# Flamingo block with a routed FFN: scaling behind the next tile's copies, order flags per distance, two buffers for the shared activations

## The reference, cut to what matters

```python
# x: 16 x 128 tokens of 256 features, ctx: 16 x 128 x 256
x = x + tanh(g_xattn) * xattn(layernorm(x), ctx)      # 16 heads of 64, one shared K/V head
                                                      # + a parallel silu(gate) * h feed-forward of 1024
x = x + tanh(g_ffn) * ffn(layernorm(x))

def ffn(x):
    shared = silu(x @ sh_up_w + sh_up_b) @ sh_down_w + sh_down_b
    scores = softmax(x @ gate_w.T)                    # 8 experts
    topk_w, topk_i = top_k(scores, 2)                 # weights normalised over the two
    for each token, each chosen expert e:
        y += w_e * (silu(x @ up_w[e] + up_b[e]) @ down_w[e] + down_b[e])     # 256 -> 256 -> 256
    return y + shared
```

## Time and profile before

| | |
|---|---|
| median of the runs | 539.51 us |
| profiled execution | 539.47 us |
| its span in the trace | 537.8 us |
| PE busy | 503.8 us (94%) |
| DVE / ACT / POOL busy | 409.4 / 327.1 / 288.5 us |
| from 446 to 524 us (78 us): PE / DVE / ACT / POOL busy | 74.25 / 57.16 / 49.04 / 55.95 us |
| granted TensorE clock in that stretch | 1.00 |
| share of the DMA engines in that stretch | 0.73 |

### The profile page before, as it was taken

How to read it: one execution, slowest core, us unless ns; L and a number is a source line. 1 busy time by engine, 2 the same in 40 slices (tenths; PEclk the granted TensorE clock), 3 DMA queues, 4 the chain that set the end, 5 groups by cost and what they waited for, 6 DMA issues and landing times.

```text
span 537.8 us, 13926 instructions
## 1 busy us (share of the span) xinstructions
PE 503.8 (94%) x4026; PEld 485.3 (90%) x4026; DVE 409.4 (76%) x1254; ACT 327.1 (61%) x1092; POOL 288.5 (54%) x330
## 2 busy tenths in 40 slices
PE   8789999999999999999999999999998889999980
PEld 7779999999999999999999999999997779889870
DVE  7687878688787878878887878787778887777760
ACT  3576656766675666566567565756665636666650
POOL 3487626454552655264355536444676315488763
PEclk9889999999999999999999999999999999999995
DMA  5551300021003000300301030023598965688853
GB/s 176 189 188 50 99 2 32 31 78 52 31 20 117 31 30 14 114 32 20 117 22 33 7 122 26 10 79 100 198 320 331 380 229 107 112 128 137 134 69 39
DMA packets 40212, 53.85 MB, mean 100 GB/s; under 512 B 4597, under 2 KB 34218, under 8 KB 39146
## 3 DMA queue, kind: packets, MB, share of 16 engines
q1 hardware_dynamic: 31856, 41.48, 23.2%
q0 software_dynamic: 8000, 11.86, 11.9%
q10 hardware_dynamic: 314, 0.01, 0.0%
HBM read 28.15 MB, written 25.21 MB: 99 GB/s over the span
## 4 chain that ended last, share of the span: by engine, by line
PE 66%; DVE 15%; issue 6%; ACT 5%; POOL 3%; DMA 2%; DVEq 1%; SPq 0%; POOLq 0%; ACTq 0%
PE bank L1523 14%; PE bank L1525 12%; PE bank L1524 12%; PE bank L1604 5%; PE bank L1709 4%; PE bank L1616 4%; PE bank L1699 4%; PE bank L1620 3%; PE bank L1607 2%; PE bank L1714 2%; PE bank L1538 2%; DVE norm_probs L988 2%; ACT norm_probs L803 1%; DMA spare<-in_L_xattn_Wq 1%; POOL weights L587 1%
## 5 line engine op out<-in xcount | busy, mean ns | idle before, releaser
L616 POOL TENSOR_TENSOR norm_probs<-norm_probs,rden 128x512 f32<-128x512 f32 x64 | 66.5, 1040 | 100.0 <-DVE rden L1168 99.2
L1523 PE MATMUL bank<-acts,weights 128*128 128x256 f32 x384 | 110.1, 287 | 3.4 <-POOL weights L587 3.4
L1524 PE MATMUL bank<-acts,weights 128*128 128x256 f32 x384 | 108.7, 283 | 0.0
L1525 PE MATMUL bank<-acts,weights 128*128 128x256 f32 x384 | 108.4, 282 | 0.0
L803 ACT ACTIVATE norm_probs<-bank,nmax 128x128 f32<-128x128 f32 x256 | 90.4, 367 | 23.4 <-DVE nmax L1124 23.4
L621 POOL TENSOR_TENSOR acts<-uf,acts 128x256 fp32r<-128x256 f32 x64 | 47.5, 741 | 68.7 <-ACT acts L791 68.7
L1523 PEld LDWEIGHTS bank<-acts,weights 128*128 128x128 f32 x384 | 73.3, 191 | 4.1 <-issue 3.0
L727 POOL DMA_INDIRECT out_x<-norm_probs,th x39 | 60.8, 1558 | 29.3 <-ACT norm_probs L916 16.7
L1525 PEld LDWEIGHTS bank<-acts,weights 128*128 128x128 f32 x384 | 73.2, 191 | 0.0
L1524 PEld LDWEIGHTS bank<-acts,weights 128*128 128x128 f32 x384 | 73.1, 190 | 0.0
L791 ACT ACTIVATE acts<-uf 128x256 fp32r<-128x256 f32 x64 | 26.8, 418 | 61.8 <-DVE uf L1193 61.7
(11 more groups left out here) (250 smaller groups left out, 1567.1 us busy)
## 6 DMA issues: line engine op xcount, KB each, us to landing
parked<-stage SPq DMA_DIRECT2D x12, 512.0 KB, 3.5
weights<-parked SPq DMA_DIRECT2D x6, 1024.0 KB
slot_rows<-tf SPq DMA_DIRECT2D x8, 680.0 KB, 6.5
spare<-slot_rows SPq DMA_DIRECT2D x39, 136.0 KB
ct<-in_ctx SPq DMA_DIRECT2D x8, 256.0 KB, 2.7
xs<-in_x SPq DMA_DIRECT2D x8, 256.0 KB, 4.5
stage<-in_L_ffn_up_w SPq DMA_DIRECT2D x8, 256.0 KB, 2.8
stage<-in_L_ffn_down_w SPq DMA_DIRECT2D x8, 256.0 KB, 3.1
```

The source lines that it names most:

```text
L616: pool.tensor_tensor(pr[:, s % 2], pr[:, s % 2], rden[:, s % 2, :].unsqueeze(2).broadcast_to((P, 4, P)), ALU.mult).then_inc(probs_ready, 1)
L1523: pe.matmul(ps, wts[1], mov[0], start=first, stop=False, skip_group_check=True)
L1524: pe.matmul(ps, wts[0], mov[0], start=False, stop=False, skip_group_check=True)
L1525: return pe.matmul(ps, wts[0], mov[1], start=False, stop=last, skip_group_check=True)
```

## The change

Line numbers in the diff are those of the files; behind the last attention group and in the tile loop nearly every engine's order moves.

- ScalarE's tile step scales last but one: rows t+2, hidden t-1, then `ys` of t-3, then Silu.
- Waits that other waits imply are left out (`tile_down_filled`, `hT_filled` on ScalarE; `tile_silu_done`, most of `y_copied` on VectorE; `tile_biased`, `down_biased`, `xg_ready` from tile 3 on TensorE).
- One flag becomes two, per distance: `turns[0]` for the tile just before, `turns[1]` for the one before that, packed into a code per expert and unpacked by shifts. GpSimd loads both per tile, and waits for `y_copied` last. With the given inputs `turns[0]` is 0 everywhere, and `turns[1]` is 16 at tiles 6 and 8 (by the kernel's formula).
- `hf` has two buffers. The low part of the last shared step moves to GpSimd, behind the row sends. `expert_lo(0)` and `(1)` move one slot forward, to slots 4 and 5.
- VectorE behind attention: `hidden_lo(1)` before the logits' copy, `add_shared(0)` before the tables. The first part of the flag table, the first register load and the first two `meta` come before the first tile's bias.

```diff
-        hf = xn.rearrange("p a n -> p (a n)").rearrange("p (m n) -> p m n", m=KT)
+        hf = norm_probs.rearrange("p s (m n) -> p s m n", m=KT)
...
@@ gpsimd
-                    if s in (5, 6) and last:
-                        expert_lo(s - 5)
+                    if s in (4, 5) and last:
+                        expert_lo(s - 4)
...
+            for m in range(KT):
+                step = TPS - 1
+                pool.wait_ge(hh_done, step * KT + m + 1)
+                pool.tensor_tensor(hh[:, step % 2, 1, m, :], hf[:, step % 2, m, :], hh[:, step % 2, 0, m, :].bitcast(F32),
+                                   ALU.subtract).then_inc(last_h_ready, 1)
...
             for t in range(TILES):
-                pool.wait_ge(y_copied, t + 1)
                 if t == 1:
                     pool.wait_ge(turns_done, 1)
                 if t >= 1:
-                    due = pool.value_load(turn[0:1, t:t + 1], min_val=0, max_val=16)
+                    due_1, due_2 = [pool.value_load(turns[i][0:1, t:t + 1], min_val=0, max_val=16) for i in range(2)]
                 if t >= 3:
                     pool.wait_ge(y_added[(t - 3) % 4], 16 * ((t - 3) // 4) + 32)
                 if t >= 2:
-                    pool.wait_ge(y_added[(t - 2) % 4], due + (16 * ((t - 2) // 4) + 16))
+                    pool.wait_ge(y_added[(t - 2) % 4], due_2 + (16 * ((t - 2) // 4) + 16))
                 if t >= 1:
-                    pool.wait_ge(y_added[(t - 1) % 4], due + (16 * ((t - 1) // 4) + 16))
+                    pool.wait_ge(y_added[(t - 1) % 4], due_1 + (16 * ((t - 1) // 4) + 16))
...
+                pool.wait_ge(y_copied, t + 1)
...
@@ scalar, hidden_hi
-                    if step > 0:
-                        act.wait_ge(h_ready, step * KT + m - KT + 1)
+                    if step >= 2:
+                        act.wait_ge(h_ready, (step - 2) * KT + m + 1)
...
@@ vector, behind attention
             x1_lo(g, dn_ps[USE_X1T % 4]).then_inc(dn_freed, 1)
+            hidden_lo(1)
...
-            hidden_lo(1)
+            add_shared(0)
+            hidden_lo(2)
...
             tables()
-            hidden_lo(2)
-            add_shared(0)
-            hidden_lo(3)
             add_shared(1)
...
@@ vector, tile_step
+                if t == -1:
+                    turn_table(0)
+                    dve.wait_ge(tables_done, 2)
+                    experts_of = dve.value_load(window[0:1, 0:1])
+                    for n in range(2):
+                        pick_meta(n, n)
+                if t in (0, 1):
+                    turn_table(t + 1)
...
@@ tensor, tile_step
-                    if t >= 2:
-                        pe.wait_ge(tile_biased, t - 1)
-                    pe.wait_ge(xg_ready, t + 1)
+                    if t < 3:
+                        pe.wait_ge(xg_ready, t + 1)
...
-                    if t >= 4:
-                        pe.wait_ge(down_biased, t - 3)
```

More of the change, by code:

```diff
@@ L205, in program @@
         weight = route(4).rearrange("p (t c) -> p t c", t=2)
-        hist = [route(NE), route(NE)]
+        hist_t = route(2 * NE).rearrange("p (k e) -> p k e", k=2)
+        hist = [hist_t[:, k, :] for k in range(2)]
         weight8 = routing[:, 0:4 * NE].rearrange("p (t c e) -> p t c e", t=2, c=2)
@@ L240, in program @@
         shares = consts[0:1, 486:486 + WIN_TILES]
-        late, early = consts[0:1, 494:494 + NE], consts[0:1, 502:502 + NE]
+        late_early = consts[0:1, 494:494 + 2 * NE].rearrange("p (k e) -> p k e", k=2)
+        late, early = [late_early[:, k, :] for k in range(2)]
         meta = th[:, 0:2 * TILES].rearrange("p (t n) -> p t n", n=2)
@@ L251, in program @@
         by_expert = slow_stage[0:1, 0:NTAB * (NE - 1)].rearrange("p (t e) -> p t e", e=NE - 1)
-        turn_f, floor_0, floor_1, shared_turn = [slow_stage[0:1, 320 + 48 * i:320 + 48 * i + (NE if i else NTAB)]
-                                                 for i in range(4)]
+        turn_f = slow_stage[0:1, 320:320 + NTAB]
+        turn_code = consts[0:1, 326:326 + NTAB].bitcast(I32)
+        floor, near = [slow_stage[0:1, 368 + 16 * i:368 + 16 * (i + 1)].rearrange("p (k e) -> p k e", k=2) for i in range(2)]
+        far, code = [slow_stage[0:1, 400 + 8 * i:408 + 8 * i] for i in range(2)]
+        turns = [slow_stage[0:1, 416 + 48 * i:416 + 48 * i + NTAB].bitcast(I32) for i in range(2)]
         count_i, count_t = slots8[0:1, 0, 0, :], slots8[0:1, 0, 1, :]
@@ L370, in program @@
         h_ready = sem("h_ready")
+        last_h_ready = sem("last_h_ready")
         dn_filled = sem("dn_filled")
@@ L1503, in tile_step @@
                                       hsT[0][(c + 1) % 2][:, :, :].bitcast(F32), ALU.subtract).then_inc(hT_ready, 1)
-                if runs(t + 2):
-                    e = dve.snap((experts_of >> (SHIFT * (k + 4))) & (NE - 1))
-                    dve.tensor_copy(meta[:, t + 2, :], rows_g[:, (c + 2) % 4, bass.ds(e * 2 + D, 2)]
-                                    ).then_inc(meta_ready, 1)
+                if t < 0:
+                    add_shared(3, (t + 2,))
+                if t == -1:
[6 more added lines that the diff above has]
+                    turn_table(t + 1)
+                if t >= 0 and runs(t + 2):
+                    pick_meta(t + 2, k + 4)
                 if runs(t - 2):
```

80 lines of the change are left out of this document (41 added, 39 removed).

## The result

The changed kernel took 543.17 us (median of 20 runs, 541.27 to 546.09); the kernel before took 539.95 beside it (20 runs). The ratio is 1.0059, 95% interval 1.0046 to 1.0073: slower by 0.6%. The forecast was 533.1, its range 531.0 to 537.3. The profiled execution took 542.22 with a span of 540.0.

What follows compares the result with a forecast made beforehand. Bound: the tile loop's ScalarE-VectorE ring, 2.05 us a step, GpSimd's scatters second. Tile 5 at 448.2, plus 33 x 1.95, 8.7 tail and 0.5: last scatter 521.8, 6.4 earlier; 539.5 - 6.4 = 533.1 us, range 531.0 to 537.3.

Steps and rivals of the forecast that it cites:

- Part 1, the pace: Tile loop: scaling behind both copies brings 2.15 us per tile to 1.95, 6.7 us less over 33 tiles.
- Part 2: Waits left out because other waits imply them: costed at nothing, at most 0.1 us in all.
- Part 3, the flags: GpSimd's scatters: distance-1 waits at tiles 5 and 8 go, 6.2 us; new waits at tiles 6 and 8 cost 2.8.
- Part 3, the second load: GpSimd's second register load per tile: taken to hide in the 1.55 us of the scatter before, cost 0.
- My other bound: GpSimd's second load: path of 1.8 us against 1.55 to hide in, so 0.15 to 0.25 per scatter.
- the equal gaps of 0.30: GpSimd: back-to-back scatters with a load lie as far apart as row sends without one, so loads hide.
- The rival with it, at 537.0: Second load on GpSimd shows in part: 0.15 per scatter, period 2.01, 537.0 us; chance 0.16.
- Part 4, the slots: Last attention group: moving GpSimd's subtractions one slot forward ends a TensorE stall, net 0.7 us less; bounds +0.3 and -1.0.
- Part 5: Behind attention: TensorE's 1.72 us stall goes but gives nothing; 0.2 later, stores may slow first row loads by up to 0.8.
- Part 6, the entrance: Front of tile loop: VectorE's flag work, load and copies delay the first bias; 0.8 us later at tile 5, bounds 0 and 1.8.
- first bias later than 441.5: Sign in the changed profile that would count against the forecast; VectorE's first bias was expected near 440.2.
- Two chains of equal length: Last scatter at 521.3 by TensorE's chain, 521.2 by GpSimd's; 0.5 us added for the tie.

Runs made afterwards that it cites:

- one_load: Changed kernel with one register load per tile on GpSimd instead of two, the distance-1 flag being a constant 0; 537.44 us (ratio 0.9968).
- old_flags: Changed kernel without register loads in the scatter loop, constant flags making tiles 5 and 8 wait for both t-1 and t-2, as before; 542.31 us (1.0047).
- slots_alone: shared_back with GpSimd's weight subtractions of the last attention group at slots 4 and 5 instead of 5 and 6; 535.22 us (0.9907).
- slots_back: packed_back with GpSimd's weight subtractions of the last attention group back at slots 5 and 6; 537.91 us (0.9965).
- shared_back: packed_back with the whole order of the shared experts' part as before, slots 5 and 6 included; 535.25 us (0.9911).
- meta_back: Changed kernel with the tile loop's entrance order as before: VectorE's load, first copies and flag table, and TensorE's load; 540.78 us (1.0012).
- packed_back: Changed kernel with both flags in one word, so one GpSimd load per tile, and meta_back's entrance order; 536.19 us (0.9924).
- loop_only: Kernel before with only ScalarE's new tile-loop order and the left-out waits of the change; 539.02 us (0.9987).

## Why the prediction was wrong

The dates of the sum against those of the changed kernel: tile 4's scatter 455.2, measured 459.95 (+4.75); from tile 4 to tile 8 10.2, measured 10.64 (+0.44); 30 scatters 55.8, measured 59.91 (+4.1); less the 0.6 by which the forecast's last scatter lay above GpSimd's own 521.2. That is the 8.7 by which the last scatter missed its date (521.8, measured 530.50). The tail was 9.5 for the 9.64 taken. The rest to 10.1 is the span's surroundings (2.2 for 1.67) and the profiled execution lying 0.95 below its median. Of the 4.75, 3.9 are TensorE's entrance (tile 5's up-projection at 452.06, forecast 448.2), and the remaining 0.9 is the second load again, by the 8.53 against one_load's 7.59.

- **Part 1, the pace: right.** 1.95 expected, 1.90 measured. The sum gained nothing by it, as GpSimd bound the end.
- **Part 2: nothing speaks against it.** No row shows a wait in place of what was left out; it was not tried by itself.
- **Part 3, the flags: right.** Waits of 5.84 and 4.80 between starts for 5.11 each; the sum had 6.2 - 2.8 = 3.4 us for them, old_flags gives 4.8, uncertain by 1.3.
- **Part 3, the second load: the step that failed.** It was taken at 0 and cost 0.14 a tile, 4.1 us behind tile 8 by the profile and 4.9 in all by the ratios of the changed kernel and one_load. I read 1.1 to 1.2 us of loads against 1.55 to hide in, and left out what else stands in that queue: an estimated 0.93 of waits and register work. My other bound, 1.8 of path against 1.55, came close (0.15 to 0.25); the equal gaps of 0.30 on which I decided tell only that one load fits, not how much room is left. The rival with it, at 537.0, had the mechanism and a chance of 0.16, but stood on my early entrance.
- **Part 4, the slots: wrong in sign** by the profile, -0.7 expected, +0.4 to +0.9 measured; slots_alone finds nothing of it in the time, and slots_back even the reverse.
- **Part 5: the direction was right, the size not.** The stall of 1.72 gave nothing, as forecast. What I priced as up to 0.8 on the first loads was a first wait for rows of 0.8 to 4.1 in the kernels with this order, where shared_back has none and 0.27 for its second tile: the products that had covered the first load were done already, and the second load was longer.
- **Part 6, the entrance: the term that was mis-sized.** 0.8 at tile 5 was expected, with a bias near 440.2; the bias came at 442.41. VectorE took 4.10 us from its last addition to that bias for 0.73 before, so 3.4 more where I had 2.3; the load alone was 1.45, not 0.6. From the bias to tile 5's up-projection I had 8.0, since the flag work was to leave that stretch, and it took 9.65 (9.34 before, 9.77 in meta_back at a clock of 1.00 and with the flag work in it). Whether the lower clock, which was not in the sum, used up the relief is not shown. meta_back gives 2.5 us back. Ahead of the run I had set "first bias later than 441.5" as a sign against me, and it was one.
- **Two chains of equal length** were expected, TensorE's and GpSimd's. In fact GpSimd's was alone: what TensorE gained beyond it was worth nothing, while a late entrance still reached the end, since it dates the first scatter.

What the ratios give, in order: the second load 0.0091 (4.9 us, uncertain by 1.4), the entrance of the loop 0.0044 (2.4, one_load to packed_back, uncertain by 1.8), the shared part's order 0.0013 (0.7, within its uncertainty). shared_back at 535.2 is still 2.1 above the forecast; single long gaps between scatters, 1.82 and 1.10 in its profile, hold 2.3 above the 0.30 of the others.

## What to carry to other kernels

An operation that "hides" tells nothing of how much more would: add up all that the queue does in the shade, and test it with one too many, since the cost stays zero until the shade is full and each further one is then paid nearly whole. A register load is such an operation; put several small values into one word, and put the load where its engine waits anyway, not in front of the first instruction of a chain. And when an engine is kept from waiting by moving its work forward, ask what that work had been covering. Compare dates of two profiles from a common event: here they shift by up to 2.3 us as a whole.

## What the runs showed of the hardware

- A third register load per tile added 0.535 us to GpSimd's period, a second one 0.09 to 0.14 and the first nothing, as the queue worked on them while a scatter ran; on VectorE a load stood bare with an idle of 1.45.
- TensorE's clock fell to its lower level after an idle of 3.21 us, and was 0.56 in the mean from 445 to 450 us. A cost in the date of the first scatter could not be seen.
- A wait whose releaser is named as a DMA can be a register load: the gaps of the changed kernel were put down to a scatter's DMA in 30 of 39 cases. Of its 38 gaps 29 were above 0.33; with one load fewer, 6 were. The chain of waits named the load's line beside the landings.
- A scatter that waits for the landing of the one just before it started 4.73 to 6.44 us after it: 5.11 and 4.85 in the kernel before, 5.39 and 5.28 in loop_only, 4.73 and 6.44 in old_flags. What makes the spread was not found.
